# Six unread products ahead of the wait for the head's exponentials, in four slots of sixteen

## The reference

```python
x = x + tanh(g_xattn[0]) * cope_attention(ln(x), ctx)   # 16 heads of 16, contextual position embedding
x = x + tanh(g_ffn[0])   * experts(ln(x))               # 8 experts, top 2, and a shared one, swiglu
x = x + tanh(g_xattn[1]) * cross_attention(ln(x), ctx)  # 16 heads, softmax(q k^T) v
x = x + tanh(g_ffn[1])   * gated_attention(ln(x))       # 16 heads, normalised q, top-3 head gates
```

```python
gates = sigmoid(logits)
pos = minimum(flip(cumsum(flip(gates))), npos_max - 1)
bias = logits_ceil * w + logits_floor * (1.0 - w)      # gathered from query @ pos_emb, w = pos - floor(pos)
scores = softmax(logits + bias)
```

## Time and profile before

| | |
|---|---|
| median of 3 runs | 5130.43 us |
| profiled execution, its own time | 5137.21 us |
| span of its trace | 5135.5 us |
| granted TensorE clock, mean over the span | 0.722 |
| TensorE busy, weight load busy | 67%, 44% |
| VectorE, ScalarE, GpSimd busy | 78%, 47%, 27% |
| DMA | 8 GB/s over the span |

### The profile page before, as it was taken

The page is one execution under the profiler, slowest core; times in us unless marked ns, Lnnn a source line. Parts: engine busy times, 40 slices in busy tenths (PEclk is TensorE's granted clock), DMA queues, the critical chain, the costliest instruction groups (busy, mean ns, idle before and its releaser), DMA issues.

```text
span 5135.5 us, 64542 instructions
## 1 busy us (share of the span) xinstructions
PE 3439.1 (67%) x21126; PEld 2246.7 (44%) x21126; DVE 3981.5 (78%) x8619; ACT 2429.6 (47%) x5505; POOL 1385.9 (27%) x1125
## 2 busy tenths in 40 slices
PE   3347676766767667676766767667675766767676
PEld 2125354453535435354443535435363443635363
DVE  3699787787978778787887978778797887978753
ACT  2454544545444444444545445444544545455432
POOL 0342322323232232222223222232322223232200
PEclk7558686686867768687686957768586776867686
DMA  4000000000000000000000000000000000000000
GB/s 124 13 5 1 1 11 1 11 1 3 9 1 11 1 11 1 1 11 1 11 1 8 4 1 11 1 11 1 1 11 1 11 1 11 1 1 7 1 7 3
DMA packets 42691, 40.93 MB, mean 8 GB/s; under 512 B 6468, under 2 KB 42342, under 8 KB 42360
## 3 DMA queue, kind: packets, MB, share of 16 engines
q1 hardware_dynamic: 42360, 36.85, 2.3%
HBM read 32.64 MB, written 4.19 MB: 7 GB/s over the span
## 4 chain that ended last, share of the span: by engine, by line
DVE 44%; PE 24%; ACT 14%; issue 13%; POOL 2%; DVEq 0%; POOLq 0%; ACTq 0%; DMA 0%; SPq 0%
DVE banks L725 8%; DVE row_negmax L1265 5%; DVE u L954 4%; PE banks L364 4%; DVE masks L716 4%; PE banks L286 4%; PE banks L273 3%; DVE eg_eth L972 3%; DVE c L687 3%; PE banks L295 2%; DVE o L981 2%; PE banks L328 2%; DVE steps L741 2%; PE banks L802 2%; ACT core_prob L579 2%
## 5 line engine op out<-in xcount | busy, mean ns | idle before, releaser
L725 DVE COPY_PREDICATED banks<-masks,banks 128x448 f32<-128x448 int16 (+5 forms) x1536 | 1030.8, 671 | 35.9
L630 POOL TENSOR_TENSOR steps<-slope,rises 128x512 f32<-128x512 f32 x256 | 301.0, 1176 | 2722.5 <-DVE masks L716 2562.2
L802 PE MATMUL banks<-xn,w 128*128 128x256 f16 x6912 | 872.2, 289 | 88.2 <-ACT h L874 58.3
L802 PEld LDWEIGHTS banks<-xn,w 128*128 128x128 f16 x6912 | 703.0, 104 | 254.9 <-ACT h L874 67.4
L716 DVE TENSOR_SCALAR masks<-shift 128x512 int16<-128x512 int16 x1536 | 334.7, 289 | 156.5 <-ACT shift L556 152.3
L687 DVE TENSOR_TENSOR_SCAN c<-gate,cap 128x514 f32<-128x514 f32 x256 | 371.7, 1452 | 88.2 <-POOL neg_rest L640 87.1
L1265 DVE TENSOR_REDUCE row_negmax<-banks 128x4 f32<-128x1024 f32 x256 | 299.9, 1217 | 141.4 <-PE banks L349 141.4
L815 PE MATMUL banks<-w,a 128*128 128x256 f32 x1152 | 299.7, 407 | 80.2 <-DVE o L981 80.2
L644 POOL TENSOR_TENSOR partial<-partial,core_scores 128x512 f32<-128x512 f32 x256 | 350.4, 1369 | 0.1
L640 POOL TENSOR_TENSOR neg_rest<-shift,c 128x512 f32<-128x512 bf16 x256 | 295.9, 1156 | 183.1 <-ACT shift L568 105.7
L874 ACT ACTIVATE h<-banks,b 128x256 f32<-128x256 f32 x576 | 239.6, 467 | 198.4 <-PE banks L802 197.8
(11 more groups left out here) (262 smaller groups left out, 7686.5 us busy)
## 6 DMA issues: line engine op xcount, KB each, us to landing
stage<-in_L_ffn_w SPq DMA_DIRECT2D x16, 512.0 KB, 5.5
ahead<-in_ctx SPq DMA_DIRECT2D x32, 128.0 KB, 2.2
ahead<-in_x SPq DMA_DIRECT2D x32, 128.0 KB, 2.3
u<-in_ctx SPq DMA_DIRECT2D x32, 128.0 KB
x<-in_x SPq DMA_DIRECT2D x32, 128.0 KB
out<-x SPq DMA_DIRECT2D x32, 128.0 KB, 1.8
stage<-in_L_ffn_w SPq DMA_DIRECT2D x8, 256.0 KB, 6.1
stage<-in_L_ffn_sw SPq DMA_DIRECT2D x2, 512.0 KB, 4.2
```

Source lines behind the costliest of these rows:

```text
L630: nc.gpsimd.tensor_tensor(k.steps[:, g % 2], k.slope[:], k.rises[:, g % 2], ALU.mult)\
L725: move = nc.vector.copy_predicated(tab[:, :, 0:S - b], k.masks[:, n, :, 0:S - b], tab[:, :, b:S])
L802: last = nc.tensor.matmul(k.bank[bank][:, f * S:(f + 1) * S], w[:, e, a, c, par, f * P:(f + 1) * P], k.x_parts[:, b, c, :], start=(n == 0) ...
```

## The change

TensorE gets six matrix products in the slots q = 9, 10, 14 and 15, behind that slot's F pieces and the waits for bank 3, and ahead of the wait for the head's exponentials. Each takes a 128 by 128 block of w1 as weights and 512 columns of w3 as moving operand, both float16, and writes all of bank 3, each over the last; the four transposes that follow overwrite the bank. No engine reads the products. The wait for the exponentials is moved behind two other waits of the same engine; no other engine's stream is changed.

```diff
 LAG = 4
+WEIGHING = (9, 10, 14, 15)
+UNREAD = 6
...
         g = s - 2
         if 0 <= g < G:
-            pe.wait_ge(sem["core_exp"], NT * (g + 1))
             if g >= 1:
                 pe.wait_ge(sem["core_pT_ready"], g)
             if g >= 4 and g % 4 == 0:
                 pe.wait_ge(sem["core_o_ready"], g // 4)
+            if (s - H - LAG) % H in WEIGHING and s >= H + LAG:
+                for _ in range(UNREAD):
+                    nc.tensor.matmul(k.bank[3][:], k.w1[:, 0, 0, 0, 0, 0:P],
+                                     k.w3[:, 0, 0, 0].rearrange("p t f -> p (t f)"), start=True, stop=True)
+            pe.wait_ge(sem["core_exp"], NT * (g + 1))
             transpose_tokens(nc, k, k.bank[3], k.core_prob).then_inc(sem["core_pT_psum"], 1)
```

## The result

The changed kernel takes 5152.24 us (median of 8 runs, 5146.08 to 5152.64) against 5131.08 us for the kernel before in the same runs: ratio 1.0036, interval 1.0025 to 1.0047. It is slower, as forecast, but by 18 us and not by 64. The 18 us are the ratio's; the two medians are 21 us apart.

What follows compares the result with a forecast made beforehand. No single engine bounds it; the four slots wait for TensorE's transposes, mostly at its low clock. 29 pairs by 0.7 + 1.5 = 2.2 us give 64 us: 5130.4 + 64 = 5194 us, range 5112 to 5240.

Steps and rivals of the forecast that it cites:

- place B: Slots q = 10 and 15: products cost 2.2 us, later pieces gain 0.7, net +1.5 us a pair.
- place A: Slots q = 9 and 14: products cost 1.9 us, later pieces gain 1.2, net +0.7 us a pair.
- whatever makes that `shift` later makes the end later by as much: ScalarE's `shift` releases VectorE's masks after 152.3 us of idling in all; any delay there was said to reach the end.
- Its 32 places: Where VectorE idles before its masks: said to be twice per sequence, behind q = 9 and 14, 4.8 us each.
- a rule on continuous work: Skill's advice to keep TensorE continuously busy; by it q = 14 would be at high clock, but the trace showed 0.50.
- the last three (1.73 us) in four of ten: After q = 9 and 14: next heads, their weighing and the head behind gain 1.73 us in four of ten slots, 0.7.
- the fifth taken off: In q = 9 and 14: gains cut by about a fifth, 0.3 us, for slots already at the high clock.
- The term left unpriced: Clock changes in all other slots: maybe 1 or 2 us per sequence either way, so 30 us.
- The clock holds: Rival: products in q = 9 and 14 lift the clock through the next slot's weighings; -38 us, 5092 us; 13%.
- It cancels: Rival: gains of 2.6 us in q = 9, 14 and 1.5 in q = 10, 15 offset costs; 5130 us; 12%.
- Hidden: Rival: a real wait for exponentials in the four slots would make the products cost nothing; part of another rival's 12%.
- No lift in time: Rival: all six products run at the low clock and lift nothing useful; +145 us, 5275 us; 7%.

Runs made afterwards that it cites:

- e6_cover: Kernel before, with unread products in the side pieces instead, five and six ahead of the waits for the first and last four weighed heads' exponentials: 0.9786, 5028.06 us.
- e5_thin: Changed kernel with the same six products in all four slots, but 32 rows instead of 128: 1.0402, 5343.78 us.
- e3_first: Changed kernel with the six products only in slots q = 9 and 14: 0.9992, 5127.91 us.
- e7_keep: e6_cover with three more unread products in q = 9 and 14, where TensorE waits for `slope`: 0.9780, 5018.38 us.
- e11_three: e3_first with three products in place of six: 0.9994, 5132.41 us.
- e9_q15: Changed kernel with the six products only in slot q = 15: 1.0028, 5150.94 us.
- e4_second: Changed kernel with the six products only in slots q = 10 and 15: 1.0044, 5154.38 us.

## Why the prediction was wrong, and where it was right

**Right:** the products have no cover. The wait they stand ahead of is met already, the whole of their time is in the stretches W2 to T1 and W4 to T2, and T1 passes it on to the masks (200.8 us of idling against 152.3). Placed in a real wait, they cost nothing (e6_cover). That the wins come from the clock is shown by e5_thin. The mostly low price and the mean clock (0.758, forecast 0.75) were right, and the four transposes ran wholly or mostly at the high level in 52 of 58 slots, 9 before. The direction was right because of place B; place A, which I had at +0.7 us a pair, came out at -0.2.

**A premise that was wrong**, though the sum hardly used it: "whatever makes that `shift` later makes the end later by as much". e3_first makes `shift` later by 35 us in all and the end by nothing. For the same reason the masks' idle time (+48.5 us, forecast +20) is no measure of the change. Its 32 places aren't two per sequence either: before the change the slots behind q = 9 and 14 have 29 of them, 5.2 us each. And q = 14 at 0.50 doesn't speak against a rule on continuous work, since TensorE was busy for 12.36 of its 15.41 us (80%, where the dense stretch of the earlier trace rows had 89%).

**Price.** From the starts in the trace six cost 2.41, 2.49, 1.69 and 2.53 us in q = 9, 10, 14 and 15, 132 us in all. I took 1.9 and 2.2, 119 us. In q = 9 the clock nearly always rises only at their end: in 13 of 15 sequences the six took 2.48 to 2.53 us. In q = 14 it was high from their start in 9 of 14 (1.30 us) and rose near their end in the others. Mis-sized a little. In the cross pair W2 to T1 grew by 0.40 us more than the products took and in the gated pair by 0.48 less: the second weighing, ahead of them, was high in 8 of 15 cross pairs before and in 1 after, and in 1 of 14 gated pairs before and in 9 after. That is luck with where the clock changes, and it nearly cancels.

**The step that failed** is the gain at place A: "the last three (1.73 us) in four of ten", and the fifth taken off, 1.2 us in all. It was 0.25 + 0.38 + 1.20 = 1.83 us in a cross pair and 0.48 + 0.97 + 1.26 = 2.71 in a gated one, 2.26 on the mean, and that is 29 x 1.06 = 31 us of the 48 by which the forecast missed the profiled execution (64 against 16); the prices, the second weighings and the gain at B come to nothing together, and 18 us are outside the pairs (below).

I read in the earlier trace rows that the clock was lost by the third weighing and took it for the rule. There TensorE had reached the high clock with the weighings alone. Behind six dense products it has it through the table, the heads and the third weighing in nearly every pair: from W3 to W4 14 of 15 cross pairs take 7.28 us (8.57 before) and all 14 gated ones 7.01. That dense work shortly ahead matters is shown the other way by e6_cover, which has the high clock at the transposes and no products between W2 and the third weighing: 8.57 us in the cross pair, and 7.53 with three in the wait for `slope` (e7_keep). But three in place of six at T1 don't do it (e11_three, 8.49), and six do it in only 8 of 15 cross pairs where place B has none (e3_first). What decides between these is open.

**Place B.** Price 2.46 and 2.54 against my 2.2; gains 0.44 + 0.48 = 0.92 us and 0.64 + 0.39 + 0.28 = 1.31 against my 0.7. Net +1.5 in a cross pair and +1.2 in a gated one; I had +1.5. Right on the mean. With A at +1.0 and -1.5 this is the pair sum, 1.16 us on the mean where I had 2.2.

**The term left unpriced**, where the clock changes in all other slots, came out at -15.4 us in q = 7 and -2.5 us in the rest, within the 30 us that I had given it. e9_q15 ties it to the products in q = 15; how they act on a slot eight further on, other than by where the clock changes, no run shows.

**The rivals.** "The clock holds" had the mechanism for A right, with its mark (heads and third weighing high), and 13% was too little; its price was wrong since the fourth weighing stayed as it was (high in 7 of 29 pairs before and after), and since B costs 2.5 us and not 1.31. I had said that a mean of L364 under 500 ns would decide; it is 517. "It cancels" came nearest in time: its mark was within 0.3% and the measured change is 0.36%. Its gains, 2.6 us at A and 1.5 at B, were 2.26 and 1.11. "Hidden" is out: up to T1 and T2 the products show in full. "No lift in time" is what e5_thin is, and it costs 206 us and not 145, since it also loses the clock that was there. TensorE's busy time fell by 59 us where I forecast a rise of 80 to 140. That is only in part the same error: the four slots account for 10 us of the fall, and 40 us lie in q = 2 and 3, which TensorE went through at a higher clock (0.99 against 0.89 in q = 2) and which took as long as before.

## What to carry to other kernels

Work that is there to raise TensorE's clock belongs where that engine idles for another one, ahead of the wait that ends last, and not behind it: the same kind of product cost 18 us behind and won 2.1% ahead. Before pricing such a place, look whether the wait it stands ahead of is ever the last (the timeline of the engine that signals it), and test with products of fewer rows, which here took the same time and lifted nothing. When the clock's level is part of the price, a single stretch at the high level that ends isn't the rate at which it is lost; and a change of one slot moves slots that it doesn't touch, so a stretch in one experiment isn't the stretch in another, although the times themselves add up within their intervals here (8 + 7 and -4 + 23 us against 18, and 14 + 9 against the 23 of e4_second). And an engine's idle time measures a change only where its next work decides the end of the stage.

## What the runs showed of the hardware

Six products with 32 rows take as long as with 128: 0.427 us from start to start at the low level in both, and 2.67 us of the chain in both. With 32 rows the mean granted clock fell from 0.722 to 0.705, with 128 it rose to 0.758. Slots with the same work took 20.6 or 21.6 us on the mean (q = 7), by full-row products issued eight slots earlier; thin ones left them at 21.68. After the change 13 of 14 sequences took 307.1 to 307.3 us; before they took from 300.2 to 308.0 us.
